# Column sums of an attention matrix moved from ScalarE's accumulator to VectorE, and partly to GpSimd

## The chip, the core and the metric

The kernel runs on one core of a Trainium2 chip. A core has five engines with instruction streams of their own: TensorE (PE, with its weight loads PEld), VectorE (DVE), ScalarE (ACT), GpSimd (POOL) and SyncE (SP), which here only issues transfers. They meet through semaphores. The metric is the time of the whole program on the device, in microseconds.

## What is computed

The layer is a pre-norm block for x of shape (2, 2048, 256): attention with 16 heads of 16 columns, then a layer norm and a mixture of 16 routed experts (two per row) and 2 shared ones. The attention part is what the change touches:

```
cos        = einsum('bhsd,bhtd->bhst', q, k)              # q, k of length 1
attn_score = (1 + arccos(clip(cos))) ** (-3.2)
n_r        = sum(attn_score, axis=-1)
n_c        = sum(attn_score, axis=-2)
k_tilde    = attn_score / n_r / n_c
out        = (k_tilde / sum(k_tilde, axis=-1)) @ v
```

The scores are kept with the key on the partition and the query along the row. The sum along a row of a tile is then n_c of its 128 keys. It is needed before the values can be divided by it, and so before any product with the scores.

## The kernel before

The program has three blocks one after the other. The first normalizes x and makes q, k and v (to about 250 us). The second, which the change touches, computes the scores and their products with the values (250 to about 5017 us). The third finishes half of the expert layer.

**Batches.** The second block goes through 64 batches, n = 4 k + m, with k from 0 to 15 and m from 0 to 3. A batch is half of the keys of one head: BT = 8 tiles of 128 keys by 2048 queries, in one of the two halves of the buffer `X` (`X[:, m % 2]`). `periods` writes the order: k = 0 to 7 is the first half, k = 8 (`SIDE`) to 15 (`LAST`) the second, whose batches are called with `beside == "tail"`. k = 1 to 4, 5 to 7 and 9 to 14 are loops on each engine.

**One batch, step by step.**
- PE computes cosines into two PSUM buffers of 1024 columns (`pieces`, L799). DVE clips them into X (`clip`, L928, 16 instructions of 1024 columns).
- POOL squares each of the 8 tiles in place (`square`, L1114).
- ACT takes `Ln` of one minus the square (`logs`, L1138, two instructions of 4 tiles) and a `Sigmoid` (`halves`, L1146, four of 2 tiles).
- PE computes the same cosines again and DVE multiplies them in (`mult`, L942, 16 instructions; the first needs the first sigmoid).
- ACT takes `Arctan` (`angles`, L1154, pieces of 4, 2 and 2 tiles, each of which needs its tiles' products), `Ln` (L1162, all 8 tiles) and `Exp` (L1168, one instruction for each tile, with `accum_out` that leaves the sum of the row in `ncol`). The score semaphore rises after tile 4 and after tile 8 (`EXP_PIECES`).
- DVE makes `1 / ncol` (L951) and the scaled values (L953) for each piece (`values`).
- PE adds the products of values and scores to one PSUM bank (`add`, L824, 8 tiles of 4 column blocks). After an odd m, DVE copies the bank out (L1085) and SP stores it.

**Order on each engine.** Each stream is in order. In the turn of batch n:
- ACT: Ln and Exp of n, then logs, sigmoids and arctangents of n+1.
- DVE: `values(n, 0)`, `values(n, 1)`, the products of n+1, the copy, the clips of n+2, then side work.
- PE: the cosines of tile 0 of n+1, the `add`s of n, the cosines of tiles 1 to 7 of n+1, the cosines for the clips of n+2, then side work.
- POOL: the squares of n+2. The squares of n+1 belong to the turn before.

**Side work of the second half.** For 256 rows in each k the expert layer of the first sequence runs beside the attention. On DVE it follows the clips: `side_residual` (m = 0, L979 to L988), `side_normal` (m = 1, L995 to L1011), `side_choose` (m = 2, L1021 to L1035) with `side_gather` of experts' chunks 0 to 3 (L1049), and the other chunks at m = 3. ACT waits for its result at one place in the turn of m = 2, after the exponentials: L1181 needs `side_l_ok` from L1011. PE's `side_work` at m = 2 waits for `side_gate` (L1033) before the experts' products (L840).

Of the kernel before, what the change touches and what calls it, by code (L numbers as in the profile page):

```python
# [5 lines left out]
def pre_ln_arccos_attention_moe_kernel(nc, x, w_qkv, b_qkv, w_out, b_out, centroids, expert_biases,  # L6
# [6 lines left out]
    fp32 = mybir.dt.float32  # L13
    bf16 = mybir.dt.bfloat16
    ALU = mybir.AluOpType
    ACT = mybir.ActivationFunctionType
    AX = mybir.AxisListType

    B, S, D = x.shape
    P = 128  # L20
# [4 lines left out]
    BT = KT // 2  # L25
# [10 lines left out]
    POWER = -2.0 - 1.2  # L36
# [17 lines left out]
    with ctx:  # L54
        def sb(name, shape, dt):
            return ctx.enter_context(nc.sbuf_tensor(name, shape, dt))
# [4 lines left out]
        def sem(name):  # L61
            return ctx.enter_context(nc.semaphore(name))


        X = sb("X", [P, 2, BT, S], fp32)
# [3 lines left out]
        ncol = sb("ncol", [P, BT], fp32)  # L69
# [14 lines left out]
        small2 = sb("small2", [P, 256], fp32)  # L84
        ident = sb("ident", [P, P], fp32)
        identb = sb("identb", [P, P], bf16)
        consts = sb("consts", [P, 4], fp32)
        one_c, theta_c, eps_c = consts[:, 0:1], consts[:, 1:2], consts[:, 2:3]

# [84 lines left out]
        def wait(engine, semaphore, value):  # L174

            if not isinstance(value, int) or value > 0:
                engine.wait_ge(semaphore, value)
# [383 lines left out]
        square_ok = sem("square_ok")  # L561
        log_ok = sem("log_ok")
        half_ok = sem("half_ok")
        atan_ok = sem("atan_ok")
        log2_ok = sem("log2_ok")
        score_ok = sem("score_ok")
        nc_ok = sem("nc_ok")
        vp_ok = sem("vp_ok")
# [9 lines left out]
        SIDE = (LAST + 1) // 2  # L578
# [106 lines left out]
        def has(k, m):  # L685

            return not (isinstance(k, int) and 4 * k + m >= NB)

        with nc.Block() as block:
# [230 lines left out]
            def _(dve):  # L920
# [20 lines left out]
                        part = X[:, m % 2, i, j * CW:(j + 1) * CW]  # L941
                        nc.vector.tensor_tensor(part, ps_cos[j % 2], part, ALU.mult).then_inc(cos_ok, 1)  # L942

                def values(k, m, piece):

                    n = 4 * k + m
                    a, b = EXP_PIECES[piece]
                    dve.wait_ge(score_ok, n * len(EXP_PIECES) + piece + 1)

                    wait(dve, sum_ps, (n - 1) * BT + b)  # L950
                    nc.vector.reciprocal(vp[:, a:b, HD:HD + 1].rearrange("p t o -> p (t o)"), ncol[:, a:b]).then_inc(nc_ok, 1)  # L951
                    dve.wait_ge(nc_ok, n * len(EXP_PIECES) + piece + 1)
                    nc.vector.tensor_tensor(vp[:, a:b, 0:HD],  # L953
                                            V[:, bass.ds(2 * k + m // 2, 1), m % 2 * BT + a:m % 2 * BT + b, :].rearrange(
                                                "p o t d -> p (o t) d"),
                                            vp[:, a:b, HD:HD + 1].broadcast_to([P, b - a, HD]), ALU.mult).then_inc(vp_ok, 1)
# [116 lines left out]

                def emit(k, m, beside):
                    for piece in range(len(EXP_PIECES)):
                        values(k, m, piece)
                    if has(k, m + 1):
                        for i in range(BT):
                            mult(k, m + 1, i)
                    if m % 2 == 1:  # L1080
                        head = 2 * k + m // 2
                        dve.wait_ge(sum_ps, (head + 1) * KT)

                        wait(dve, head_stored, head * 16)
                        nc.vector.tensor_copy(evac[:, :], ps_sum).then_inc(sum_ok, 1)  # L1085
                    if has(k, m + 2):
                        for i in range(BT):
                            clip(k, m + 2, i)
                    if beside == "weights":
                        weights(k, m)  # L1090
                    if beside == "tail":
                        if m == 0 and isinstance(k, int) and k == SIDE:
                            side_scales()
                            assert steps[0] == SCALE_STEPS
                        elif m == 0:
                            steps[0] = SCALE_STEPS + (k - SIDE) * PAIR_STEPS
                        side_work(k, m)
                        side_gather(k, *CHUNKS.get(m, (0, 0)))
                        if m == 3 and isinstance(k, int) and k == SIDE:
                            assert steps[0] == SCALE_STEPS + PAIR_STEPS  # L1100
# [8 lines left out]
            @block.gpsimd  # L1109
            def _(pool):  # L1110
                def square(k, m, i):
                    pool.wait_ge(cos_ok, clips(4 * k + m, i))
                    own = X[:, m % 2, i, :]
                    nc.gpsimd.tensor_tensor(own, own, own, ALU.mult).then_inc(square_ok, 1)  # L1114

                def emit(k, m, beside):
                    if has(k, m + 2):
                        for i in range(BT):
                            square(k, m + 2, i)


                hold(pool, square_ok, BT)
                for i in range(BT):
                    square(0, 1, i)
                periods(pool, emit)

            @block.scalar
            def _(act):
                def tiles(m, a, b):
                    return X[:, m % 2, a:b, :]  # L1130

                def logs(k, m):

                    n = 4 * k + m
                    for a, b in LOG_PIECES:
                        act.wait_ge(square_ok, n * BT + b)
                        own = tiles(m, a, b)
                        nc.scalar.activation(own, own, ACT.Ln, bias=one_c, scale=-1.0).then_inc(log_ok, 1)  # L1138

                def halves(k, m):  # L1140

                    n = 4 * k + m
                    act.wait_ge(log_ok, (n + 1) * len(LOG_PIECES))
                    for a, b in HALF_PIECES:
                        own = tiles(m, a, b)
                        nc.scalar.activation(own, own, ACT.Sigmoid, scale=-0.5).then_inc(half_ok, 1)  # L1146

                def angles(k, m):

                    n = 4 * k + m  # L1150
                    for a, b in ATAN_PIECES:
                        act.wait_ge(cos_ok, mults(n, b - 1))
                        own = tiles(m, a, b)
                        nc.scalar.activation(own, own, ACT.Arctan).then_inc(atan_ok, 1)  # L1154

                def scores(k, m):

                    n = 4 * k + m
                    nc.scalar.preload_act_table_set("natural_log_exp_and_others")
                    act.wait_ge(atan_ok, (n + 1) * len(ATAN_PIECES))  # L1160
                    own = tiles(m, 0, BT)
                    nc.scalar.activation(own, own, ACT.Ln, bias=theta_c, scale=-2.0).then_inc(log2_ok, 1)  # L1162
                    act.wait_ge(log2_ok, n + 1)
                    for piece, (a, b) in enumerate(EXP_PIECES):
                        wait(act, vp_ok, n * len(EXP_PIECES))
                        for i in range(a, b):
                            own = X[:, m % 2, i, :]
                            last = nc.scalar.activation(own, own, ACT.Exp, scale=POWER, accum_out=ncol[:, i:i + 1])  # L1168
                        last.then_inc(score_ok, 1)

                def emit(k, m, beside):
                    scores(k, m)
                    if beside == "tail" and m == 1:

                        act.wait_ge(side_var, (k - SIDE + 1) * 2)
                        nc.scalar.activation(s_log, s_mean[:, :, 1], ACT.Ln, bias=eps_c).then_inc(side_log, 1)
                        act.wait_ge(side_log, k - SIDE + 1)
                        nc.scalar.activation(s_inv, s_log, ACT.Exp, scale=-0.5).then_inc(side_inv, 1)
                    if beside == "tail" and m == 2:
                        act.wait_ge(side_l_ok, k - SIDE + 1)  # L1180
                        nc.scalar.activation(s_exp, s_exp, ACT.Exp).then_inc(side_exp, 1)  # L1181
                    if has(k, m + 1):
                        logs(k, m + 1)
                        halves(k, m + 1)
                        angles(k, m + 1)

                for i in range(BT):
                    act.wait_ge(cos_ok, clips(0, i))
                    own = X[:, 0, i, :]
                    nc.scalar.activation(own, own, ACT.Square).then_inc(square_ok, 1)  # L1190
                logs(0, 0)
                halves(0, 0)
                angles(0, 0)
                periods(act, emit)


# [414 lines left out]
```

## Time and profile before

| | us |
|---|---|
| median of 3 runs | 5336.46 |
| lowest and highest run | 5336.09, 5336.95 |
| profiled execution, its own time | 5337.28 |
| profiled execution, its span | 5335.6 |
| ACT busy | 4923.4 |
| DVE busy | 3274.6 |
| PE busy | 3097.5 |
| POOL busy | 1808.4 |

The span goes from the first to the last instruction; 1.7 us of the execution's own time lie around it. Busy times are sums over the whole span. A row of the timeline gives the start, the time taken, the engine, the line and the operation, and merges instructions that follow each other closely (xcount is their number); the bracket gives how long the engine had been idle and what ended that.

### The profile page before, as it was taken

Reading aid. Unit: us, or ns where it says so; the run is one execution under the profiler, and the core shown is the slowest. Engines: PE = TensorE matmul, PEld = TensorE weight load, DVE = VectorE, ACT = ScalarE, POOL = GpSimd, SP = SyncE. Lnnn points to the kernel's source line nnn. Section 1 sums busy time; section 2 is a strip of 40 time slices with the busy share of each in tenths; the row PEclk is TensorE's granted clock in tenths of the full one; section 3 lists DMA queues with packets and bytes.
Section 4 is the critical chain, followed back from the end, with each engine's and each line's share of the span. In section 5 each row is a group of like instructions: output and inputs, shape, how many; then the busy total and the mean of one; then the engine's idle time right before and its main releaser. Section 6 shows DMA issues by size and latency. Waiting matters only on the chain. (4 is left out here: it accounts for less than half of the span.)

```text
span 5335.6 us, 38170 instructions
## 1 busy us (share of the span) xinstructions
PE 3097.5 (58%) x10678; PEld 796.3 (15%) x10678; DVE 3274.6 (61%) x3861; ACT 4923.4 (92%) x2159; POOL 1808.4 (34%) x545
## 2 busy tenths in 40 slices
PE   7635565554444555444546657565655656565699
PEld 4200010000000000000001102111111111111244
DVE  7735665556545565545657676666767576666466
ACT  5799999999999999999989999999999999999521
POOL 0224433444334443334424443344333443334000
PEclk9866655667866656667566857686777668576799
DMA  2100000000000000000000101010010101010200
GB/s 87 63 8 14 18 14 14 14 18 18 14 18 16 12 10 10 6 6 10 12 29 24 36 10 52 2 51 10 30 32 24 36 10 51 7 47 2 82 28 16
DMA packets 71843, 128.14 MB, mean 24 GB/s; under 512 B 9654, under 2 KB 46937, under 8 KB 71706
## 3 DMA queue, kind: packets, MB, share of 16 engines
q1 hardware_dynamic: 70554, 122.50, 7.3%
q0 software_dynamic: 1152, 4.19, 0.3%
q14 instruction: 98, 0.80, 0.1%
q8 instruction: 39, 0.64, 0.0%
HBM read 96.77 MB, written 29.88 MB: 24 GB/s over the span
## 5 line engine op out<-in xcount | busy, mean ns | idle before, releaser
L1114 POOL TENSOR_TENSOR X<-X 128x2048 f32<-128x2048 f32 x504 | 1799.9, 3608 | 3001.3 <-DVE X L928 3001.3
L799 PE MATMUL psum<-stacks 128*128 128x512 bf16 x4096 | 1749.5, 524 | 1397.4 <-DVE X L942 1021.4
L942 DVE TENSOR_TENSOR X<-psum,X 128x1024 f32<-128x1024 f32 x1024 | 1194.3, 1218 | 1057.8 <-ACT X L1146 1046.5
L928 DVE TENSOR_SCALAR X<-psum 128x1024 f32<-128x1024 f32 x1024 | 1186.0, 1215 | 16.6 <-PE psum L799 13.9
L1168 ACT ACTIVATE X<-X 128x2048 f32<-128x2048 f32 x512 | 969.9, 1895 | 6.9
L1146 ACT ACTIVATE X<-X 128x4096 f32<-128x4096 f32 x256 | 904.8, 3604 | 0.7
L1138 ACT ACTIVATE X<-X,consts 128x8192 f32<-128x8192 f32 x128 | 903.7, 7107 | 0.0
L1154 ACT ACTIVATE X<-X 128x4096 f32<-128x4096 f32 (+1 forms) x192 | 897.8, 4739 | 2.7 <-DVE X L942 2.7
L1162 ACT ACTIVATE X<-X,consts 128x16384 f32<-128x16384 f32 x64 | 892.8, 13951 | 0.8
L824 PE MATMUL psum<-X,vp 128*32 128x512 f32 x4096 | 569.2, 715 | 474.1 <-DVE vp L953 473.8
L799 PEld LDWEIGHTS psum<-stacks 128*128 128x128 bf16 x4096 | 260.0, 105 | 2885.0 <-DVE X L942 1847.7
L951 DVE RECIPROCAL vp<-ncol 128x4 f32<-128x4 f32 x128 | 23.0, 180 | 580.2 <-ACT X L1168 542.2
L824 PEld LDWEIGHTS psum<-X,vp 128*32 128x32 f32 x4096 | 140.3, 129 | 885.8 <-issue 532.2
L840 PE MATMUL psum<-V,u_t 128*128 128x512 f32 (+1 forms) x576 | 255.7, 603 | 0.0
L1378 PE MATMUL psum<-X 128*128 128x512 f32 (+1 forms) x576 | 246.4, 578 | 0.0
L1049 DVE SCALAR_TENSOR_TENSOR rows<-psum,gate,rows 128x256 f32<-128x256 f32 x256 | 123.9, 484 | 115.2 <-PE psum L840 110.6
L1545 DVE SCALAR_TENSOR_TENSOR X<-psum,X 128x256 f32<-128x256 f32 x240 | 104.5, 479 | 75.9 <-PE psum L1378 70.9
L840 PEld LDWEIGHTS psum<-V,u_t 128*128 128x128 f32 x576 | 115.4, 203 | 136.5 <-issue 109.0
L1378 PEld LDWEIGHTS psum<-X 128*128 128x128 f32 x576 | 106.5, 191 | 112.5 <-issue 98.4
L953 DVE TENSOR_TENSOR vp<-V,vp 128x64 f32<-128x64 f32 x128 | 105.8, 826 | 19.4 <-DVE vp L951 18.6
L523 PE MATMUL psum<-X 128*128 128x512 f32 (+1 forms) x256 | 101.8, 521 | 0.7 <-ACT X L324 0.7
L1168 ACT ACTIVATION_READ_ACCUMULATOR X<-X 128x1 f32 x512 | 95.4, 186 | 0.0
(165 smaller groups left out, 1347.4 us busy)
## 6 DMA issues: line engine op xcount, KB each, us to landing
V<-expert_w SPq DMA_DIRECT2D x64, 512.0 KB, 3.6
stacks<-qk_parts SPq DMA_DIRECT2D x256, 64.0 KB
qk_parts<-X SPq DMA_DIRECT2D x96, 128.0 KB, 1.9
stacks<-qk_parts SPq DMA_DIRECT2D x64, 192.0 KB
head_out<-evac SPq DMA_DIRECT2D x32, 256.0 KB, 2.1
expert_w<-u_t SPq DMA_DIRECT2D x17, 256.0 KB, 2.6
X<-in_L_attn_x_dram POOLq DMA_DIRECT2D x8, 512.0 KB, 4.3
stacks<-qk_parts SPq DMA_DIRECT2D x32, 128.0 KB
```

The lines of the kernel that those rows point to most:

```text
L799: return nc.tensor.matmul(dst, stacks[:, 1, buf, keys:keys + P], stacks[:, 0, buf, q0:q0 + n], start=True, stop=True)
L824: mm = nc.tensor.matmul(ps_sum[32 * j:32 * j + 32, :], vp[:, i, :], X[:, m % 2, i, j * 512:(j + 1) * 512], start=(m % 2 == 0 and i == 0), ...
L840: mm = nc.tensor.matmul(dst, u2_t[:, h, kc, :], w_ring[c % 3][:, kc, 0:wide], start=(kc == 0), stop=(kc == KC - 1 and wide == 2 * D))
L928: nc.vector.tensor_scalar(X[:, m % 2, i, j * CW:(j + 1) * CW], ps_cos[j % 2], -CLIP, CLIP, ALU.max, ALU.min).then_inc(cos_ok, 1)
L942: nc.vector.tensor_tensor(part, ps_cos[j % 2], part, ALU.mult).then_inc(cos_ok, 1)
L1114: nc.gpsimd.tensor_tensor(own, own, own, ALU.mult).then_inc(square_ok, 1)
L1138: nc.scalar.activation(own, own, ACT.Ln, bias=one_c, scale=-1.0).then_inc(log_ok, 1)
L1146: nc.scalar.activation(own, own, ACT.Sigmoid, scale=-0.5).then_inc(half_ok, 1)
L1154: nc.scalar.activation(own, own, ACT.Arctan).then_inc(atan_ok, 1)
L1162: nc.scalar.activation(own, own, ACT.Ln, bias=theta_c, scale=-2.0).then_inc(log2_ok, 1)
L1168: last = nc.scalar.activation(own, own, ACT.Exp, scale=POWER, accum_out=ncol[:, i:i + 1])
L1378: mm = nc.tensor.matmul(dst, u_t[j % 2][:, kc, :], we_t[c][:, kc, :], start=(kc == 0), stop=(kc == KC - 1 and wide == 2 * D))
```

## The change

A buffer `folded` and two semaphores are added. In the first half ACT takes the exponential of 4 tiles in one instruction without the accumulator, and DVE sums each piece of 4 tiles with one `reduce_sum` of 128 x 4 x 2048 in `values`. In the second half ACT does the same for the first piece (tiles 0 to 3). POOL then adds the halves of each of those tiles (`fold`: 1024 elements, then 512, in fp32), and DVE sums what remains, 4 x 512 elements a row. The second piece (tiles 4 to 7) keeps one instruction for each tile with the accumulator. `fold(n)` stands on POOL ahead of the squares of n+2 and so behind the squares of n+1.

```diff
+        folded = sb("folded", [P, BT // 2, S // 2], fp32)
+        sums_ok = sem("sums_ok")
+        fold_ok = sem("fold_ok")
...
-                def values(k, m, piece):
+                def values(k, m, piece, own):
...
                     dve.wait_ge(score_ok, n * len(EXP_PIECES) + piece + 1)
+                    if own == "scores":
+                        nc.vector.reduce_sum(ncol[:, a:b], X[:, m % 2, a:b, :], AX.X).then_inc(sums_ok, 1)
+                    elif own == "folded":
+                        dve.wait_ge(fold_ok, (n - SIDE * 4 + 1) * (b - a) * 2)
+                        nc.vector.reduce_sum(ncol[:, a:b], folded[:, :, 0:S // 4], AX.X).then_inc(sums_ok, 1)
+                    else:
+                        dve.sem_inc(sums_ok, 1)
+                    dve.wait_ge(sums_ok, n * len(EXP_PIECES) + piece + 1)
...
-                        values(k, m, piece)
+                        values(k, m, piece, "scores" if beside != "tail" else ("folded", "")[piece])
...
+                def fold(k, m):
+                    n = 4 * k + m
+                    done = (n - SIDE * 4) * BT
+                    a, b = EXP_PIECES[0]
+                    pool.wait_ge(score_ok, n * len(EXP_PIECES) + 1)
+
+                    wait(pool, sums_ok, (n - 1) * len(EXP_PIECES) + 1)
+                    for i in range(a, b):
+                        own = X[:, m % 2, i, :]
+                        nc.gpsimd.tensor_tensor(folded[:, i - a, :], own[:, 0:S // 2], own[:, S // 2:S],
+                                                ALU.add).then_inc(fold_ok, 1)
+                        pool.wait_ge(fold_ok, done + 2 * (i - a) + 1)
+                        part = folded[:, i - a, 0:S // 4]
+                        nc.gpsimd.tensor_tensor(part, part, folded[:, i - a, S // 4:S // 2], ALU.add).then_inc(fold_ok, 1)
+
                 def emit(k, m, beside):
+                    if beside == "tail":
+                        fold(k, m)
                     if has(k, m + 2):
                         for i in range(BT):
                             square(k, m + 2, i)
...
                     for piece, (a, b) in enumerate(EXP_PIECES):
-                        wait(act, vp_ok, n * len(EXP_PIECES))
+                        if beside != "tail" or piece == 0:
+                            own = tiles(m, a, b)
+                            nc.scalar.activation(own, own, ACT.Exp, scale=POWER).then_inc(score_ok, 1)
+                            continue
+
+                        act.wait_ge(vp_ok, n * len(EXP_PIECES))
                         for i in range(a, b):
                             own = X[:, m % 2, i, :]
                             last = nc.scalar.activation(own, own, ACT.Exp, scale=POWER, accum_out=ncol[:, i:i + 1])
                         last.then_inc(score_ok, 1)
```

## Rows read from the trace of the kernel before

**Rows 1.** The page: busy time of each engine.

```profile
PE 3097.5 (58%) x10678; PEld 796.3 (15%) x10678; DVE 3274.6 (61%) x3861; ACT 4923.4 (92%) x2159; POOL 1808.4 (34%) x545
```

**Rows 2.** Timeline of ACT, one batch of the first half.

```profile
1498.38 14.13 ACT L1146 ACTIVATE X<-X 128x4096 f32<-128x4096 f32 x4
1512.43 14.03 ACT L1154 ACTIVATE X<-X 128x8192 f32<-128x8192 f32 x3
...
1541.85 1.91 ACT L1168 ACTIVATE X<-X 128x2048 f32<-128x2048 f32 x1
...
1557.00 14.12 ACT L1138 ACTIVATE X<-X,consts 128x8192 f32<-128x8192 f32 x2
```

**Rows 3.** Timeline of all engines, another batch of the first half.

```profile
2001.28 14.12 ACT L1138 ACTIVATE X<-X,consts 128x8192 f32<-128x8192 f32 x2
...
2020.50 18.83 DVE L942 TENSOR_TENSOR X<-psum,X 128x1024 f32<-128x1024 f32 x16 [18.39 <-ACT X L1146]
...
2030.75 14.03 ACT L1154 ACTIVATE X<-X 128x8192 f32<-128x8192 f32 x3
...
2039.85 18.73 DVE L928 TENSOR_SCALAR X<-psum 128x1024 f32<-128x1024 f32 x16
...
2042.27 28.50 POOL L1114 TENSOR_TENSOR X<-X 128x2048 f32<-128x2048 f32 x8 [46.05 <-DVE X L928]
...
2060.16 1.91 ACT L1168 ACTIVATE X<-X 128x2048 f32<-128x2048 f32 x1
...
2070.99 8.85 PE L824 MATMUL psum<-X,vp 128*32 128x512 f32 x64 [11.32 <-DVE vp L953]
```

**Rows 4.** Timeline of POOL, DVE and ACT around a batch m = 3.

```profile
4067.05 28.50 POOL L1114 TENSOR_TENSOR X<-X 128x2048 f32<-128x2048 f32 x8 [46.10 <-DVE X L928]
...
4085.45 1.91 ACT L1168 ACTIVATE X<-X 128x2048 f32<-128x2048 f32 x1
...
4092.07 0.19 DVE L1028 TENSOR_REDUCE small<-small 128x2 f32<-128x32 f32 x1
4092.29 3.30 DVE L1029 TENSOR_TENSOR small<-small 128x32 f32<-128x32 f32 x1
4095.63 0.19 DVE L1031 SCALAR_TENSOR_TENSOR small<-small 128x32 f32<-128x32 f32 x1
...
4097.44 0.19 DVE L1033 TENSOR_TENSOR gate<-small 128x32 f32<-128x32 f32 x1
...
4115.30 0.18 DVE L951 RECIPROCAL vp<-ncol 128x4 f32<-128x4 f32 x1 [0.27 <-DVE rows L1049]
...
4123.59 15.93 DVE L942 TENSOR_TENSOR X<-psum,X 128x1024 f32<-128x1024 f32 x14 [1.40 <-PE psum L799]
...
4130.50 14.04 ACT L1154 ACTIVATE X<-X 128x8192 f32<-128x8192 f32 x3 [0.33 <-DVE X L942]
```

**Rows 5.** Timeline of PE: the products with the scores at m = 3 and m = 0.

```profile
4115.94 7.07 PE L824 MATMUL psum<-X,vp 128*32 128x512 f32 x64 [1.09 <-DVE vp L953]
...
4180.31 8.77 PE L824 MATMUL psum<-X,vp 128*32 128x512 f32 x64 [3.56 <-DVE vp L953]
```

**Rows 6.** Waits in total, times, longest: ACT's, DVE's of the second half.

```profile
ACT small L1181 <- DVE small L1011: 6.1, 8, 1.1
...
DVE X L942 <- PE psum L799: 9.7, 7, 2.2
...
DVE vp L951 <- issue: 15.0, 5, 3.4
```

**Rows 7.** Timeline of ACT and DVE, exponentials of m = 2 and the side work.

```profile
4010.78 1.91 ACT L1168 ACTIVATE X<-X 128x2048 f32<-128x2048 f32 x1
...
4021.76 0.69 DVE L1004 TENSOR_TENSOR rows<-rows,V 128x512 f32<-128x512 f32 x1
```

**Rows 8.** Timeline of the last batch of the second block.

```profile
4979.76 1.91 ACT L1168 ACTIVATE X<-X 128x2048 f32<-128x2048 f32 x1
...
4999.10 14.86 PE L840 MATMUL psum<-V,u_t 128*128 128x512 f32 x36
```

More of the change, by code:

```diff
@@ L1154, in angles, with scores @@
                         nc.scalar.activation(own, own, ACT.Arctan).then_inc(atan_ok, 1)
-                def scores(k, m):
+                def scores(k, m, beside):
                     n = 4 * k + m
@@ L1171, in emit @@
                 def emit(k, m, beside):
-                    scores(k, m)
+                    scores(k, m, beside)
                     if beside == "tail" and m == 1:
```

## The prediction

> **What bounds the kernel now.** I read the page first. ACT is busy for 4923 of 5336 us, the next engine for 3275 [rows 1], so the question is where ACT's stream is held up. ACT's timeline of a first-half batch shows no gap: one kind of instruction follows the other [rows 2]. A shorter exponential stage there is a shorter kernel, as long as nothing else arrives late. The timeline of all engines gives those others' slack, and the timelines of the second half show that at two places the slack is gone: at m = 3 the arctangents wait 0.33 us for VectorE's products, whose tile 1 had waited 1.40 us for TensorE [rows 4] (such waits of VectorE for L799 came 7 times in the second half, once in each k that has a next batch), and at m = 2 ACT waits for the side work's logits all 8 times, 6.1 us together [rows 6]. Whatever comes later there costs ACT directly.
>
> **Part 1: ACT's saving.** Before, the eight exponentials take 1557.00 - 1541.85 = 15.15 us, 1.894 each. Four sigmoids, which have no accumulator to read, go through the same elements in 1512.43 - 1498.38 = 14.05. Three arctangents (8192 + 4096 + 4096) last 14.03 where the four sigmoids last 14.13, so an instruction fewer is 0.10 less [rows 2]. Two exponentials of 8192 then take 14.05 - 0.20 = 13.85: 1.30 us saved a batch, 32 x 1.30 = **41.6 us** in the first half. In the second, four exponentials become one: 7.57 becomes 6.93, 0.65 a batch (at most 21 us), and only where ACT isn't waiting.
>
> **Part 2: first half, what VectorE adds.** Take the start of a batch's exponentials as 0. Piece 0 is ready at 6.9, piece 1 at 13.85. The trace has no long sum from SBUF. Nearest is a clip, 18.73 / 16 = 1.17 us for 1024 elements [rows 3], 1.14 ns an element, which bounds 8192 above at 9.4 us. From 512 elements (L1004, 0.69 [rows 7]) to 1024 it is 0.48 more, 0.94 ns an element, which bounds it below at 7.7. I take 8.6, between them. VectorE's last clip ended 2060.16 - 2058.58 = 1.6 us before 0 [rows 3], so it is free: sum 7.0 to 15.6, values ready 16.3; second sum to 24.9, values at 25.6 (27.2 at the upper bound). The second four tiles' products take half of 8.85 [rows 3], or up to 7 if all of them ran at half the speed of [rows 5]: done by 30 to 33. They are needed when? ACT starts the logs at 13.85; products with the cosines start 2020.50 - 2001.28 = 19.2 later, 33.1; tile 1 is needed 2.4 later and TensorE needs 0.6 for it (end of the adds, 4123.01, to 4123.59 [rows 4, 5]): 34.9. The arctangents start 29.5 after the logs, 0.9 later than tile 3 is ready [rows 3], so the limit for ACT is 35.8. Covered by 2 us or more. Without that cover each us late is a us of ACT, 32 times. Cost taken: 0. VectorE's sums run while GpSimd squares (to 2070.77, 10.6 on this scale [rows 3]). A reduction started under a running square took 0.19 us (L1028), a two-input operation right behind it 3.30 (L1029), ending with the square [rows 4], so I charge the sums nothing for this.
>
> **Part 3: the fold's length.** A square of 2048 takes 28.50 / 8 = 3.56 us [rows 3]. In proportion 1024 takes 1.78 and 512 takes 0.89; with some 0.1 fixed each, and 0.2 for the second one's wait on the first, a tile is 3.1 and a batch 12.4 us (bounds 10.7, with nothing fixed, and 14). GpSimd is in order: the squares of n+1 end at 10.1 to 11.0 (4095.55 - 4085.45 at m = 3 [rows 4]), so the fold runs from there to about 23, not from 6.9. By the Trainium skill (GPSIMD Engine Reference, section "Performance versus the Vector engine") a two-input add of 2048 fp32 takes 4497 ns; the squares here take 3560 [rows 3], and by the page's figure the fold would be 13.5 us plus waits.
>
> **Part 4: second half, m = 0 and m = 1.** Fold ended at 23.0 (m = 1) or 23.5; reduction of 2048 elements 2.2; reciprocal and values 0.6: products start at 26.0 to 26.4. All eight tiles are now behind this, since piece 1 queues behind piece 0 on VectorE and TensorE. After an idle stretch they take about 8.8 [rows 3, 5]: ended at 35 to 36. The limit is 14.5 + 19.2 + 2.4 - 0.6 + 0.9 = 36.4. Just covered: m = 1 keeps -0.65. At m = 0 VectorE shows up to 3.4 us that nothing explains at the loop's return [rows 6]; if GpSimd has such a pause too, the fold starts later and ACT waits 0 to 3. I take 1.0: +0.35 net. Eight of each: -5.2 and +2.8.
>
> **Part 5: m = 2.** ACT waits for L1011, so its 0.65 buys nothing. Behind the last square stands now the fold. L1004, with two SBUF inputs, starts 4021.76 - 4010.78 = 11.0 [rows 7] and meets the first fold instruction as L1029 meets a square [rows 4]: about +1 (until 12.0), and up to +3 if L1000 meets it as well. Part is hidden by L1006's own wait for TensorE. I take +1.5, eight times: **+12**.
>
> **Part 6: m = 3, the largest term.** `side_choose` runs from 2.7 before 0. Each of its two-input operations waits for the running square. After the last square, at 10.1, the rest (L1031 to L1033) took 2.0 us [rows 4]. Now the fold begins exactly there, and six two-input operations remain, alternating with fold instructions of 1.9 and 1.0. If each is caught, that is 3 x 1.9 + 3 x 1.0 less what they overlap, about 6.9; if they slip through the pauses before each second fold instruction, about 3.6. Bounds 0 and 8.7; I take 5.5. The gate is late by that, and with it TensorE's `side_work` queued on it, the gather, and `values(n, 0)` (4115.30, 29.9 on this scale). There the fold has long ended, but its reduction stands on the path: 2.3. TensorE's idle gap ahead of the products grows from 1.09 to 3.4 us; after 3.56 idle they took 8.77 instead of 7.07 [rows 5], after 11.32 idle 8.85 [rows 3]: +1.8. Nothing covers this: products of tile 1, the arctangents and all of ACT follow. 5.5 + 2.3 + 1.8 = 9.6, seven times (k = 8 to 14): **+67.2**. The saved 0.65 is lost in the wait. The Trainium skill says of this (SBUF — State Buffer, section "Who interferes with whom") that VectorE with two SBUF inputs and a GpSimd instruction that reads SBUF exclude each other for the whole instruction, whoever issues second, and that a reduction doesn't contend on this chip. The trace agrees (3.30 against 0.19 us). Read as strictly as the page has it, all six are caught and the term is 6.9, the sum 10 us more.
>
> **Part 7: the end.** The last batch has no squares ahead: fold 7.0 to 19.4, reduction and values to 22.3, eight tiles about 9: 31.5. Before, they were done at 4999.1 - 4979.8 = 19.3 [rows 8]. TensorE's last expert products and the third block follow: **+12**.
>
> **Sum.** -41.6 + 2.8 - 5.2 + 12 + 67.2 + 12.2 = +47.4 us. Against the profiled execution (5335.6 of span, 1.7 around it, 5337.3) that is 5384.7; it lay 0.8 above the median, so the runs should give 5384.
>
> **Rivals.**
> - *VectorE slips through (faster).* If GpSimd's waits between fold instructions let the small operations in, the gate isn't late, m = 2 costs 0, and m = 3 pays only reduction and TensorE's slower products: 2.3 + 1.7 = 4.0. Sum: -41.6 - 5.2 - 5.2 + 0 + 28 + 12.2 = -11.8, 5325. For it: each second fold instruction waits on the first. Against it: between squares a waiting VectorE operation ends exactly with the square and the next square catches the next one (4092.29 + 3.30). It decides where the port costs nothing at m = 3; from 0.2 us on it is no change, from 3 us on a loss. Chance 0.12.
> - *In between*, a port cost of 0.2 to 3 us: within 10.7 us of before. Chance 0.08.
> - *The fold is long or starts late.* 14 us, or a loop pause of 3 us on GpSimd, and every operation caught: m = 0 +3, m = 1 +1, m = 2 +3, m = 3 +12.7. -41.6 + 24 + 8 + 24 + 89 + 14 = +117, 5453. Few rows bear all of this at once; 0.15 for anything above 5415.
> - *The long sums are slow.* From 1.35 ns an element the second piece's products miss 35.8 in all 32 batches; at 1.5 ns they end at 37.5 to 40 and ACT waits some 2.3 each time: 5384 + 74 = 5458. Every row of VectorE at 1024 elements is faster (1.14). Chance 0.05.
> - *My forecast*, 5345 to 5415: 0.60.
>
> **How the numbers follow.** The likeliest is 5384. The range, 5330 to 5425, takes in the case in between, part of the first rival and the lower part of the third. A change under 0.2%, 10.7 us, can't be told from none here. The case in between is no change, with 0.01 from the edges of its neighbours. Faster 0.12, same 0.09, slower 0.79.
>
> **What would show it.** After: two L1168-like exponentials of about 6.9 us in the first half, a period 1.3 shorter, no idle on ACT there; VectorE reductions of about 8.6 us. In the second half: folds starting where the squares end, small operations of `side_choose` that take 0.9 to 1.9 us after the last square instead of 0.19, L1033 about 5.5 us later from the exponentials' start, arctangents of m = 3 waiting about 10 us. If ACT's waits for L942 stay under 3 us at m = 3, the step of part 6 is wrong and so is the sign.

## The result and the profile after

The changed kernel takes 5447.36 us (median of 4 runs, 5443.55 to 5448.68), the kernel before 5336.27 on the same chip: 1.0206 of it (95% interval 1.0193 to 1.0219), 111 us slower. I had forecast 5384 and a range of 5330 to 5425. The sign was right, the size was less than half of what came, and the time lies outside the range. The profiled execution took 5448.7, its span is 5446.8, 111.2 longer than that of before.

The page of the changed kernel first: busy times, the slices of ACT, and the groups that answer to [rows 1].

```profile
PE 3033.0 (56%) x10544; PEld 805.9 (15%) x10678; DVE 3922.3 (72%) x3957; ACT 4863.1 (89%) x1487; POOL 2270.3 (42%) x801
...
ACT  5799999999999999999898989999898989989421
...
L953 DVE TENSOR_REDUCE ncol<-X 128x4 f32<-128x8192 f32 x64 | 555.8, 8684 | 298.7 <-ACT X L1195 298.7
...
L1136 POOL TENSOR_TENSOR folded<-X 128x1024 f32<-128x1024 f32 x128 | 301.8, 2358 | 61.1 <-ACT X L1195 61.1
L956 DVE TENSOR_REDUCE ncol<-folded 128x4 f32<-128x2048 f32 x32 | 73.2, 2286 | 291.8 <-POOL folded L1140 289.9
...
L1140 POOL TENSOR_TENSOR folded<-folded 128x512 f32<-128x512 f32 x128 | 164.8, 1287 | 10.0
```

ACT is busy 60 us less, as it should be, and yet the span is longer: its row of slices has gaps (seven 8s, where the kernel before has one) in the second half only. What it waits for is in its waits (total, times, longest):

```profile
ACT X L1182 <- DVE X L945: 115.2, 22, 13.9
...
ACT small L1214 <- DVE small L1022: 52.9, 8, 6.7
...
ACT L1448 <- PEq L692: 39.5, 1, 39.5
```

L1182 is the arctangent (L1154 before), L1214 the side work's exponential (L1181 before, [rows 6]). They were 2.7, 6.1 and 24.5 before, the last being the time between ACT's last exponential and the third block. So ACT waits 112.5 + 46.8 + 15.0 = 174.3 us more and works 32 x 1.30 + 32 x 0.65 = 62.4 less by the prediction's figures (60.3 by the two pages): 111.9 together (114.0), against a span 111.2 longer. The account closes to within 3 us.

**First half.** Timeline of one batch of the changed kernel, to set beside [rows 2, 3]:

```profile
2027.64 13.95 ACT L1195 ACTIVATE X<-X 128x8192 f32<-128x8192 f32 x2
2034.70 8.69 DVE L953 TENSOR_REDUCE ncol<-X 128x4 f32<-128x8192 f32 x1 [8.46 <-ACT X L1195]
2041.50 14.12 ACT L1166 ACTIVATE X<-X,consts 128x8192 f32<-128x8192 f32 x2
...
2044.04 8.68 DVE L953 TENSOR_REDUCE ncol<-X 128x4 f32<-128x8192 f32 x1
...
2053.52 5.34 PE L827 MATMUL psum<-X,vp 128*32 128x512 f32 x32 [4.25 <-DVE vp L964]
...
2060.74 18.74 DVE L945 TENSOR_TENSOR X<-psum,X 128x1024 f32<-128x1024 f32 x16 [7.27 <-ACT X L1174]
2070.97 14.03 ACT L1182 ACTIVATE X<-X 128x8192 f32<-128x8192 f32 x3
```

The exponentials take 2041.50 - 2027.64 = 13.86 us instead of 15.15. The products with the scores end at 2058.9, 1.9 us before the next products start, and the arctangents have no wait in their bracket. This half went as worked out.

**Second half, m = 3.** POOL, DVE, PE and ACT around the same batch as in [rows 4]. Its exponentials start at 4124.57.

```profile
4106.18 28.51 POOL L1125 TENSOR_TENSOR X<-X 128x2048 f32<-128x2048 f32 x8 [35.72 <-DVE X L931]
4134.65 2.35 POOL L1136 TENSOR_TENSOR folded<-X 128x1024 f32<-128x1024 f32 x1
4137.07 1.27 POOL L1140 TENSOR_TENSOR folded<-folded 128x512 f32<-128x512 f32 x1
4138.30 2.35 POOL L1136 TENSOR_TENSOR folded<-X 128x1024 f32<-128x1024 f32 x1
```

```profile
4134.77 2.27 DVE L1042 SCALAR_TENSOR_TENSOR small<-small 128x32 f32<-128x32 f32 x1
4137.08 0.19 DVE L1036 TENSOR_REDUCE small<-small 128x2 f32<-128x32 f32 x1
4137.30 1.09 DVE L1037 TENSOR_TENSOR small<-small 128x32 f32<-128x32 f32 x1
4138.43 2.28 DVE L1038 TENSOR_TENSOR small<-small,order 128x32 f32<-128x32 f32 x1
4140.74 0.19 DVE L1039 TENSOR_REDUCE small<-small 128x2 f32<-128x32 f32 x1
4140.96 1.08 DVE L1040 TENSOR_TENSOR small<-small 128x32 f32<-128x32 f32 x1
4142.08 2.28 DVE L1043 TENSOR_TENSOR small<-small 128x32 f32<-128x32 f32 x1
4144.39 1.30 DVE L1044 TENSOR_TENSOR gate<-small 128x32 f32<-128x32 f32 x1
```

```profile
4166.20 8.77 PE L827 MATMUL psum<-X,vp 128*32 128x512 f32 x64 [3.53 <-DVE vp L964]
```

```profile
4182.46 14.04 ACT L1182 ACTIVATE X<-X 128x8192 f32<-128x8192 f32 x3 [13.81 <-DVE X L945]
```

The small operations end with the fold instruction that was running: 4134.65 + 2.35 = 4137.00 and 4134.77 + 2.27 = 4137.04. The two reductions between them take 0.19 each. All six two-input operations are caught. L1044 ends 21.1 us after the exponentials' start, where L1033 ended 12.2 after them: the gate is 8.9 late. The products start behind it and take 8.77, and ACT waits 13.81 where it waited 0.33.

### The profile page after: what moved, and what is told of

It is laid out like the page before. It is cut to its first block and busy times, and to the rows that moved or that the text cites. A ratio compares the mean times of both kernels' runs of the same rounds, so it can differ in the third digit from the quotient of the medians.

```text
span 5446.8 us, 37939 instructions
## 1 busy us (share of the span) xinstructions
PE 3033.0 (56%) x10544; PEld 805.9 (15%) x10678; DVE 3922.3 (72%) x3957; ACT 4863.1 (89%) x1487; POOL 2270.3 (42%) x801
## 5 line engine op out<-in xcount | busy, mean ns | idle before, releaser
L802 PE MATMUL psum<-stacks 128*128 128x512 bf16 x3962 | 1612.4, 499 | 865.2 <-DVE X L945 472.6
L827 PE MATMUL psum<-X,vp 128*32 128x512 f32 x4096 | 638.7, 787 | 1078.5 <-DVE vp L964 1078.5
L931 DVE TENSOR_SCALAR X<-psum 128x1024 f32<-128x1024 f32 x1024 | 1186.2, 1216 | 15.8 <-PE psum L802 14.3
L1182 ACT ACTIVATE X<-X 128x4096 f32<-128x4096 f32 (+1 forms) x192 | 898.2, 4741 | 115.2 <-DVE X L945 115.2
L953 DVE TENSOR_REDUCE ncol<-X 128x4 f32<-128x8192 f32 x64 | 555.8, 8684 | 298.7 <-ACT X L1195 298.7
L1195 ACT ACTIVATE X<-X 128x8192 f32<-128x8192 f32 x96 | 671.4, 7025 | 2.0
L827 PEld LDWEIGHTS psum<-X,vp 128*32 128x32 f32 x4096 | 151.5, 139 | 1545.9 <-DVE vp L964 786.7
L1136 POOL TENSOR_TENSOR folded<-X 128x1024 f32<-128x1024 f32 x128 | 301.8, 2358 | 61.1 <-ACT X L1195 61.1
L956 DVE TENSOR_REDUCE ncol<-folded 128x4 f32<-128x2048 f32 x32 | 73.2, 2286 | 291.8 <-POOL folded L1140 289.9
L1411 PE MATMUL psum<-X 128*128 128x512 f32 (+1 forms) x576 | 245.2, 576 | 0.0
L1201 ACT ACTIVATE X<-X 128x2048 f32<-128x2048 f32 x128 | 242.2, 1893 | 0.0
L1140 POOL TENSOR_TENSOR folded<-folded 128x512 f32<-128x512 f32 x128 | 164.8, 1287 | 10.0
```

The costliest lines, as they stand in the source:

```text
L802: return nc.tensor.matmul(dst, stacks[:, 1, buf, keys:keys + P], stacks[:, 0, buf, q0:q0 + n], start=True, stop=True)
L827: mm = nc.tensor.matmul(ps_sum[32 * j:32 * j + 32, :], vp[:, i, :], X[:, m % 2, i, j * 512:(j + 1) * 512], start=(m % 2 == 0 and i == 0), ...
L931: nc.vector.tensor_scalar(X[:, m % 2, i, j * CW:(j + 1) * CW], ps_cos[j % 2], -CLIP, CLIP, ALU.max, ALU.min).then_inc(cos_ok, 1)
L953: nc.vector.reduce_sum(ncol[:, a:b], X[:, m % 2, a:b, :], AX.X).then_inc(sums_ok, 1)
L1195: nc.scalar.activation(own, own, ACT.Exp, scale=POWER).then_inc(score_ok, 1)
L1411: mm = nc.tensor.matmul(dst, u_t[j % 2][:, kc, :], we_t[c][:, kc, :], start=(kc == 0), stop=(kc == KC - 1 and wide == 2 * D))
```

## The experiments

In all of them the first half is that of the changed kernel. A table inside the kernel says for each m of the second half how the two pieces are summed ("scores": DVE from X, "folded": over GpSimd's fold, "": ACT's accumulator); where it stands, lines shift by a few. The medians are of 4 runs each (e4 and e8 ran once); the kernel before took 5336.3 beside the first four, 5338.6 beside the next four and 5336.5 beside the last.

**e1_first_half.** The second half as before.

```diff
+        SUMS = [('', ''), ('', ''), ('', ''), ('', ''), ('scores', 'scores')]
```

> The first half as changed, the second as before. My theory: in the first half VectorE's long sums (8.69 us each in the trace of after) are covered, and ScalarE saves 1.3 us in each of 32 batches: 5336.3 - 41.6 = 5294.7 us, and ScalarE's waits as in the kernel before. Rival (the sums hold up something in the first half too, and only part of the loss is in the second): 5300 us or more, with waits of L945 for TensorE in the first half.

5293.52 us, ratio 0.9919 (0.9903 to 0.9936): 42.8 us faster than before, 41.6 expected. ACT waits 1.9 us for the products with the cosines and 5.9 for the side work, like the kernel before. The first half of the change is a gain by itself, and all of the loss (154 us from here to the changed kernel) is in the second.

**e2_fold_after_gate.** GpSimd starts the fold of m = 3 only after `side_choose`.

```diff
 pool.wait_ge(score_ok, n * len(EXP_PIECES) + 1)
+if m == 3:
+    pool.wait_ge(side_gate, k - SIDE + 1)
```

> The changed kernel, but at m = 3 GpSimd's fold also waits for the side work's gate, so that no fold instruction runs beside side_choose. Port theory: L1044 comes again about 12.2 us after the exponentials' start instead of 21.1, ScalarE's wait at m = 3 falls from 13.8 to about 5 us (the fold's own sum, 2.4, and slower products, 1.8, stay), 7 x 8.9 = 62 us less: 5385 us. Rival A (the sum over the folded rows and TensorE's products make the wait, not the port): 13.8 stays, 5447 us. Rival B (VectorE waits for the fold to end): the fold ends later still, so slower than 5447 us.

5378.01 us, ratio 1.0076 (1.0059 to 1.0093): 69 us less than the changed kernel. DVE's timeline beside the rows of L1042 to L1044 above, and ACT's wait:

```profile
3789.72 0.19 DVE L1046 SCALAR_TENSOR_TENSOR small<-small 128x32 f32<-128x32 f32 x1
...
3791.28 0.19 DVE L1048 TENSOR_TENSOR gate<-small 128x32 f32<-128x32 f32 x1
```

```profile
3827.58 14.05 ACT L1188 ACTIVATE X<-X 128x8192 f32<-128x8192 f32 x3 [3.99 <-DVE X L948]
```

The exponentials start at 3779.51, so the gate is there 12.0 us later. At m = 3 ACT's wait falls from 13.8 to 4.0 in most of the 7 batches, 66.6 us together (95.2 to 28.6); all its waits for L948 fall by 69.0, of which 2.4 lie at m = 0 and m = 1. Rival A gives 5447 and rival B more; both are out. What is left, 4.0, is in the main the sum over the folded rows (2.29) and TensorE's slower products (8.69 against 7.07).

**e3_fold_m01.** The fold only at m = 0 and m = 1.

```diff
+        SUMS = [('folded', ''), ('folded', ''), ('', ''), ('', ''), ('scores', 'scores')]
```

> The first half as changed; in the second the fold only at m = 0 and m = 1, the accumulator at m = 2 and m = 3. Theory: the loss sits at m = 2 and m = 3. Left are -41.6 of the first half, -0.65 x 16 of ScalarE, and ScalarE's waits of m = 0 and m = 1 (18.6 us in all in the trace of after): 5336.3 - 41.6 - 10.4 + 18.6 = 5303 us, 8 us slower than with the first half alone. Rival (the fold is worth having where no side chain runs beside it): under 5294.7 us.

5310.48 us, ratio 0.9952 (0.9936 to 0.9969). That is 17 slower than e1, and 7 above what the theory gave: ACT waits 23.6 us for L948 (18.6 taken; the changed kernel's own waits at m = 0 and m = 1 are 20.0), and 10.0 for the side work at m = 2 (5.9 in e1), although no fold runs there. So some 4 us of the loss at m = 2 come with the batches before it. The fold isn't worth having even where no side chain runs beside it. So about 137 of the 154 us come from m = 2, m = 3 and the end.

**e5_vector_direct.** DVE sums the scores of tiles 0 to 3 itself in the whole second half, with no help from GpSimd.

```diff
+        SUMS = [('scores', '')] * 4 + [('scores', 'scores')]
```

> The changed kernel without GpSimd's fold: in the second half VectorE itself sums the scores of tiles 0 to 3 (8.7 us), the other four keep the accumulator. Theory (what GpSimd does for VectorE costs more than it saves): m = 0 +0.85, m = 1 -0.65, m = 2 0 (ScalarE waits for the side work anyway), m = 3 +8.9 + 1.8 = +10.7 in 7 batches, the end +5.5, the first half -41.6: 5336.3 + 41 = 5377 us, 70 faster than the changed kernel. Rival (a VectorE already 72% busy needs the help): slower than 5447 us.

5362.70 us, ratio 1.0048 (1.0031 to 1.0065): 85 us less than with GpSimd's help, and 14 less than the theory gave. Nearly all of the 14 is m = 0, for which it had charged 0.85 us a batch, and whose batches came 0.7 shorter than before. ACT has no wait for DVE at m = 0 and m = 1, 11.8 to 12.7 at m = 3 (7 times, 83.8 us in all), 11.0 in all at m = 2. DVE's rows at m = 3 (the reciprocal of the first piece waits for the long sum):

```profile
3493.72 8.69 DVE L957 TENSOR_REDUCE ncol<-X 128x4 f32<-128x8192 f32 x1 [0.15 <-DVE rows L1064]
3502.56 0.18 DVE L966 RECIPROCAL vp<-ncol 128x4 f32<-128x4 f32 x1 [0.15 <-DVE ncol L957]
```

A sum four times as long on the engine that was said to need help is still cheaper than the fold at m = 0, 1 and 2, and 2 us cheaper at m = 3.

**e7_fold_after_both.** As e2, and at m = 2 the fold waits for the side work's logits.

```diff
 if m == 3:
     pool.wait_ge(side_gate, k - SIDE + 1)
+if m == 2:
+    pool.wait_ge(side_l_ok, k - SIDE + 1)
```

> As e2_fold_after_gate, and at m = 2 the fold waits for the side work's logits (L1026) as well. Theory: ScalarE's wait for L1026 falls from 6.7 to about 1.4, but the fold then starts at 15.8 after the exponentials' start, is 14.6 long, and TensorE's products end 4 to 5 us past their limit, so that a wait for L948 takes its place: nearly as slow, 5370 to 5378 us. Rival (the port is all of it at m = 2 too): 5.3 x 8 = 42 us less, 5336 us.

5401.39 us, ratio 1.0119 (1.0103 to 1.0136), slower than e2 and outside both expectations. The port's part went as expected: ACT's wait for L1026 fell from 52.9 to 15.7 us. But the wait that took its place is larger than I had worked out:

```profile
3448.05 14.04 ACT L1190 ACTIVATE X<-X 128x8192 f32<-128x8192 f32 x3 [5.81 <-DVE X L948]
```

At m = 2 it is 5.81 us, because the fold starts at 3412.69 and is 14.7 long, and the products after it take 10.0 us instead of the changed kernel's 9.2. The eight waits are 43.8 together, more than the 37.2 that the side work's wait gave back. The waits at m = 3, 0 and 1 rose as well, from 4.0, 1.35 and 0.95 to 5.5, 1.82 and 1.19. At m = 0 the rise is in the products, 9.01 us in e2 and 9.49 here, at a mean granted clock of 0.78 and 0.74 (TensorE, first e2, then e7):

```profile
3578.66 9.01 PE L830 MATMUL psum<-X,vp 128*32 128x512 f32 x64 [13.74 <-DVE vp L968]
```

```profile
3585.19 9.49 PE L830 MATMUL psum<-X,vp 128*32 128x512 f32 x64 [14.10 <-DVE vp L968]
```

At m = 3 the products hardly differ (8.77 against 8.69 us, the same idle gap of 3.56 before them). There the gate comes 0.4 later and the gather's first operation 1.0 later, counted from the exponentials' start, so the sum over the folded rows starts at 30.2 instead of 28.8. What held the side work up there stays open. What the run shows is that at m = 2 there is no good place for the fold: early it holds the side chain up, late its own length does.

**e4_operands.** What an instruction of the fold costs and why. At m = 0 the first one multiplies the halves, at m = 1 it adds the first half to itself, so the sums of tiles 0 to 3 there aren't those of the scores.

```diff
-nc.gpsimd.tensor_tensor(folded[:, i - a, :], own[:, 0:S // 2], own[:, S // 2:S], ALU.add)
+second = own[:, 0:S // 2] if m == 1 else own[:, S // 2:S]
+nc.gpsimd.tensor_tensor(folded[:, i - a, :], own[:, 0:S // 2], second, ALU.mult if m == 0 else ALU.add)
```

> The changed kernel, with other operands in the first instruction of the fold (sums are then not those of the scores): at m = 0 it multiplies the two halves, at m = 1 it adds the first half to itself. In the changed kernel an add of 1024 elements took 2.35 us and one of 512 1.29, 2.07 ns an element, where a square of 2048 takes 3.61, 1.76 ns. Theory (two different operands cost GpSimd more than one read twice): 2.35 stays at m = 0, about 1.9 at m = 1. Rival (the add is slower than the product): about 1.9 at m = 0, 2.35 at m = 1. Rival (a fixed cost of some 0.6 us for each instruction, whatever the operands): 2.35 at both.

GpSimd's timeline, first m = 1, then m = 0:

```profile
3971.13 1.89 POOL L1141 TENSOR_TENSOR folded<-X 128x1024 f32<-128x1024 f32 x1
...
4212.69 2.36 POOL L1141 TENSOR_TENSOR folded<-X 128x1024 f32<-128x1024 f32 x1
```

It is the operands: 1.89 us when both are the same rows, 2.36 when they differ, whatever the operation (the product here, the sum in the changed kernel). The squares, from which I had scaled the fold, read one row twice. The run (5429.07 us) also shows what the length does: with the fold of m = 1 1.9 us shorter, ACT's waits there, 7.8 us in the changed kernel, are gone, and at m = 2, where nothing was altered, it waits 46.4 us instead of 52.9.

**e8_memset.** At m = 2 and m = 3 the eight fold instructions are eight memsets of the folded rows. The sums of tiles 0 to 3 are left out there.

```diff
+if m >= 2:
+    for j in range(2):
+        nc.gpsimd.memset(folded[:, :, :], 1.0).then_inc(fold_ok, 1)
+        hold(pool, fold_ok, done + 2 * (i - a) + 1 + j)
```

> The changed kernel, but at m = 2 and m = 3 GpSimd's eight fold instructions are eight memsets that fill the folded rows (the sums of tiles 0 to 3 are left out there): GpSimd is busy in the same place and reads nothing. Theory (VectorE's second SBUF input and GpSimd's read exclude each other): side_choose's operations behind the last square take 0.19 us each beside the memsets, L1026 and L1048 come as in the kernel before, ScalarE's waits fall as in e2. Rival (any GpSimd instruction on SBUF holds VectorE up): they take as long as a memset.

The memsets took 3.5 us each, 29 in all, twice the fold, so the time (5543 us, one run) says nothing and ACT's waits rose (15.2 at m = 3: the fold's end is now what is late). What counts are DVE's rows while they run. GpSimd's memsets of m = 3 begin at 3855.54, of m = 2 at 3766.95:

```profile
3766.95 3.52 POOL L1144 MEMSET folded<- 128x4096 f32 x1
...
3855.54 3.51 POOL L1144 MEMSET folded<- 128x4096 f32 x1
```

```profile
3767.07 7.21 DVE L1015 TENSOR_SCALAR V<-rows,small 128x256 f32<-128x256 f32 x2
3774.31 0.69 DVE L1019 TENSOR_TENSOR rows<-rows,V 128x512 f32<-128x512 f32 x1
...
3855.68 0.19 DVE L1046 SCALAR_TENSOR_TENSOR small<-small 128x32 f32<-128x32 f32 x1
...
3857.26 0.19 DVE L1048 TENSOR_TENSOR gate<-small 128x32 f32<-128x32 f32 x1
```

The two-input operations run at full speed beside a memset: what they exclude is a GpSimd instruction that reads SBUF. That half of the expectation held. L1026 did not come as before, though: the two `tensor_scalar` of L1015 (L1000 before, 0.73 together) took 7.21, until the second memset's end. They have one SBUF tensor as input (and two columns of scalars), and wait for a GpSimd instruction that only writes.

**e6_combined.** No fold; DVE sums where the waits say that it is free.

```diff
+        SUMS = [('scores', ''), ('scores', 'scores'), ('', ''), ('', ''), ('scores', 'scores')]
```

> No fold at all. The first half as changed; in the second VectorE sums piece 0 itself at m = 0 and both pieces at m = 1, where e5_vector_direct showed no wait of ScalarE for VectorE, and the accumulator stays at m = 2 and m = 3. Theory (what counts is only whether VectorE's sum ends before TensorE is needed again): 8 x 0.65 + 8 x 1.3 = 15.6 us less than the first half alone, 5278 us. Rival (the second piece at m = 1 pushes the products past their limit): 5284 us or more, waits of ScalarE for L948 at m = 1.

5282.16 us, ratio 0.9898 (0.9881 to 0.9914), 4 above the theory's value. ACT waits 5.1 us for L948, 5 times: 3.7 at m = 0 (k = 12 to 14) and 1.4 at m = 3, where the kernel before has 2.7; none at m = 1, where the rival put them.

**e9_second_piece.** The same with the second piece at m = 0.

```diff
-        SUMS = [('scores', ''), ('scores', 'scores'), ('', ''), ('', ''), ('scores', 'scores')]
+        SUMS = [('', 'scores'), ('scores', 'scores'), ('', ''), ('', ''), ('scores', 'scores')]
```

> As e6_combined, but at m = 0 of the second half VectorE sums the second piece (tiles 4 to 7) instead of the first; the first has its sums from the accumulator. In e6 the values of m = 0 came 8.7 us later than the loop's return allowed, and TensorE's eight tiles all stood behind them: waits of ScalarE for L948 of 0.5 to 1.4 us, 5.1 us in all. Theory: the first four tiles' products now start under the sum, ScalarE's waits for L948 fall to about 0, some 5 us less than e6: 5277 us. Rival (the products of the second piece end past the limit all the same): as e6, 5282 us, or more.

5280.32 us, ratio 0.9895 (0.9879 to 0.9912), the lowest median of all, 3 above the theory's value. The waits for L948 fell to 3.4 us. Those at m = 0 are gone, as the theory has it; what is left is 2.5 at m = 3, which the expectation had counted to m = 0, and one of 0.9 at m = 1. Each of e6 and e9 is 56 us below the kernel before that ran beside it, and the two ratios' intervals overlap almost fully, so whether it is better than e6 isn't shown. Either is 1% faster than the kernel before.

## Why the prediction was wrong

Its steps against the runs:

| term | predicted | measured |
|---|---|---|
| first half | -41.6 | -42.8 (e1) |
| m = 0 and m = 1 | -2.4 | +9.6 |
| m = 2 | +12 | +41.6 |
| m = 3 | +67.2 | +87.9 |
| end | +12.2 | +14.3 |
| sum | +47.4 | +110.6 |

The measured column below the first row is from the two traces. For m = 3 it is the seven longest waits of L1182 (95.2 us) less 2.7 before and less 7 x 0.65. For m = 2 it is 52.9 - 6.1 - 8 x 0.65. For m = 0 and 1 it is 20.0 of waits less 16 x 0.65. The end is 15.0 less the 0.65 of the last batch. The forecast missed by 29.6 us at m = 2, 20.7 at m = 3, 12.0 at m = 0 and m = 1, and 2.1 at the end.

**Parts 1 and 2** held: 13.86 us for two exponentials (13.85 forecast), 8.68 for a long sum (8.6), nothing uncovered. (In the traces a batch of the first half is 1.37 us shorter, not 1.30: the first exponential also starts 0.09 sooner behind the start of the logarithm.)

**Part 3 is the step that failed first, and parts 4 to 7 build on it.** "In proportion 1024 takes 1.78 and 512 takes 0.89" scaled from a square that reads one row twice. The fold reads two different rows: 2.35 and 1.27 to 1.29, so 3.66 us a tile from start to start and 14.6 a batch, above my bound of 14. e4 shows the cause for the instruction of 1024: 1.89 with the same operand, 2.36 with two. The sentence on the Trainium skill (GPSIMD Engine Reference, "Performance versus the Vector engine") had the better number: by an estimate from 1.27 at 512 and 2.35 at 1024, 2048 elements would be 4.5 us, which is its 4497 ns. The row that I preferred was a different case of the same instruction.

**Part 6** had the right mechanism and the right list of what hangs on it, and the port's term was mis-sized: 5.5 taken, 8.9 measured. All six operations are caught (2.27, 1.09, 2.28, 1.08, 2.28, 1.30); I had given the slipping through half the weight. The strict reading of the Trainium skill, which part 6 priced at 6.9, was right: that is 1.4 of the 3.4. Fold instructions longer than I took them did the rest. The sum, 2.3, and TensorE's slower products, 1.7 (8.77 against 7.07), are as forecast: 8.9 + 2.3 + 1.7 = 12.9 against a wait that grew by 13.5, of which ACT's earlier arrival is 0.65. e2 shows the port's part alone (9.8 of ACT's waiting for a gate 9.1 earlier).

**Part 5** was mis-sized most: +1.5 taken, 5.2 measured (41.6 / 8; L1022 ends 21.2 us after the exponentials' start, L1011 ended 15.6 to 16.3). I had left open whether L1000 meets the fold, and took a value near the lower end. It does, and the cost lies above my upper end of 3 too. DVE's timeline of the changed kernel:

```profile
4055.54 3.75 DVE L1011 TENSOR_SCALAR V<-rows,small 128x256 f32<-128x256 f32 x2
4059.32 2.71 DVE L1015 TENSOR_TENSOR rows<-rows,V 128x512 f32<-128x512 f32 x1
```

3.75 and 2.71 instead of 0.73 and 0.69, and L1017 comes behind them. In e7, with no fold beside this chain, L1026 ends at 16.6: 4.6 us are the fold at m = 2 itself, the rest comes with the batches before (e3, e4).

**Part 4** followed part 3: with a fold 2.2 us longer, and products of mostly 9.2 to 9.6 us instead of 8.8, the products ended past the limit that I had given, and ACT waited 1.1 to 1.9 us in most of these batches. With a shorter fold the wait at m = 1 is gone (e4). GpSimd showed no pause at the loop's return: at m = 0 the fold begins as the last square ends. VectorE's of some 3 us, which comes again in e5 (up to 3.3), doesn't show here: VectorE waits for the fold at that place.

**Among the rivals**, the third (long fold, every operation caught, 5453 us) is what happened, 6 us off, with a chance of 0.15 for all above 5415. I had called it a coincidence of several things. It was two: every operation was caught, and the fold was long; its length enters the port's cost at m = 2 and m = 3, the waits at m = 0 and m = 1 and the end together, and so these terms had to be moved together in the range. That the rival's total comes so close is partly luck: it has 32 us for m = 0 and m = 1, where 9.6 came, and 24 for m = 2, where 41.6 came.

## What to carry to other kernels

Moving work off the busiest engine pays where the receiver is idle between two of its deadlines, and in this kernel that differs from batch to batch: the same sum on VectorE is free at m = 0 and m = 1 and costs 12 us at m = 3 (e5). In these traces the helper on GpSimd held up the operations of VectorE with two inputs in SBUF, and the `tensor_scalar` of the side work, that met one of its instructions; a chain of small dependent operations met all of them. Scale an instruction's cost only from a row with the same operands, and where one uncertain length enters several terms, move them together in the range.

## What was unexpected of the hardware

- GpSimd's `tensor_tensor` of 1024 fp32 elements a row takes 1.89 us when both inputs are the same rows, 2.35 when they differ.
- Two of VectorE's `tensor_scalar` of 256 elements, which take 0.73 us alone, ended with the GpSimd instruction they met: 3.75 us beside the fold, 7.21 beside memsets, which read nothing. Two-input operations ran beside such memsets in 0.19 us. The Trainium skill (SBUF — State Buffer, "Who interferes with whom") has both: that an operation with two SBUF inputs contends with a GpSimd instruction that reads and not with one that only writes, and that `tensor_scalar` can enter a mode with both ports, and so contend, when its operands allow it. The trace agrees with the first, and with the second in that the `tensor_scalar` were caught, which take 0.41 us each when alone; that they ran in that mode no run here shows.
- After an idle gap of 3.5 us TensorE's products in the changed kernel began at a mean granted clock of 0.59 (4166 to 4170 us), most of it at the lower of the two levels (0.5, which is 1.2 GHz), and went on at 0.98 (4170 to 4175), nearly all at the higher (2.4 GHz):

```profile
4166.00:4170.00 4.00, 3.80 (x23) 0.97 (x27) 2.91 (x5) 2.65 (x1) 0.00 (x0) 0.59 0.01 2
4170.00:4175.00 5.00, 4.97 (x48) 1.46 (x42) 0.00 (x0) 0.00 (x0) 0.00 (x0) 0.98 0.00 0
```

The columns are the stretch, its length, the busy time of PE, PEld, DVE, ACT and POOL, the granted clock, and the transfers' share and GB/s. A gap of 1.09 us had not cost this: there the 64 products took 7.07 us [rows 5].
